# Cross-attention: the maxima of two score tiles subtracted by four 32-row matmuls behind the product passes of both

## The chip, the cores and the metric

One core of one Trainium2 chip runs the whole kernel. The metric is the device time of one execution in microseconds (us); the median of the runs counts.

## What is computed

A decoder layer in post-norm form, float32, batch 4, 512 positions, width 256. Only the second of its three parts matters here:

```python
x = _layernorm(x + _L0_attn_ref(...))              # self-attention over the batch, and a dynamic convolution
x = _layernorm(x + _L0_xattn_ref(x, context, ...)) # cross-attention, this case
x = _layernorm(x + _L0_ffn_ref(...))               # mixture of 8 experts, 2 per token

def _L0_xattn_ref(x, context, w_q, w_kv, w_out, b_out):   # 16 heads of 64, context of 1601 rows
    q = (x @ w_q).reshape(b, n, HEADS, DIM_HEAD)
    kv = (context @ w_kv).reshape(b, m, 2, HEADS, DIM_HEAD)
    k, v = (kv[:, :, 0], kv[:, :, 1])
    attn = jnp.einsum('bnhd,bmhd->bhnm', q, k) * scale
    attn = jax.nn.softmax(attn, axis=-1)
    out = jnp.einsum('bhnm,bmhd->bnhd', attn, v).reshape(b, n, INNER)
    return out @ w_out + b_out
```

## The kernel before

The cross-attention works in 16 rounds, one for each batch and each quad of four heads. A round has two blocks, p = 0 and p = 1, one for each pair of heads. In a block the transposed scores of the pair (context rows on partitions, 512 queries in the free dimension) are made in 13 tiles of 128 context rows, t = 0 to 12; the last has 65 rows (MT, M_LAST). A tile is 2 x 512 elements wide, one PSUM bank for each head, and `ps_s` has room for two tiles, used in turn. One head of a pair lies on partitions 0 to 63 of `q` and `k`, the other on 64 to 127 (XD = 64), so each matmul of a tile uses 64 rows of the array.

Float32 products are made from rounded parts: k_hi q_hi, k_lo q_hi and k_hi q_lo. A fourth pass subtracts the row maximum of every query: `row_one` is 1 in rows 0 and 64, and `q_neg` holds the negated maxima in rows 0 and 64 and zeros elsewhere (L836 to L844). ScalarE exponentiates the tile from PSUM into one of seven `pexp` buffers (L942), TensorE multiplies it with V (PV, L856), and GpSimd adds it to `total` (L1001), from which RS (L910) makes the row sums by a matmul with ones.

All engines walk the same list of steps (`walk`), and each does its own part of a step in that order. `block` (L554) writes the list of a block; `one_round` joins two blocks and the rest:

- S (p, t): the score tile. PV (p, t): in twos behind every odd t from 3 on, for tiles t-3 and t-2; the last three tiles' at the end of the block.
- MX: matmuls of q_hi and k_hi (L887) over 402 context rows, for the maxima of the next block. VectorE reduces each (L1060, `parts`). They come in groups of two, one per head; MX_BEFORE and MX_BEHIND say how many groups stand before and behind each S: one behind every t from 1 on, one more before t = 4, 7, 10 and 12.
- SH (p): at the end of a block VectorE reduces `parts` to `negmax` (L1067), a matmul with the identity turns it (L895), and ScalarE writes `q_neg` (L972).
- K, Q, V: projections (L827), split by ScalarE (`k_hi`) and VectorE (`k_lo`). K chunks 0 and 1 and Q stand at the end of the block before, chunks 2 and 3 behind t = 1. V stands in block 1.
- R1 to R4: reciprocals of the sums (L1075), `att` (L1080), `att_hi` (L967, ScalarE, t = 8), `att_lo` (L1083, VectorE). OP: the output projection (L827) behind t = 9, added to X by VectorE (L1090).
- LDA, LDB, LDC: loads of weights and context by SyncE. WA (t = 10 of block 0), WB, CX (t = 5 and 8, only where the batch changes): their split into parts, ScalarE's `_hi` first, then `_lo` by GpSimd (or VectorE for the second half of the context).

RING_JOBS (K, Q, MX, SH, V, RS, OP) share three PSUM banks, `ps_ring`, in turn; `take_bank` waits until the job three before has been drained. Waits are on semaphores; `exp_done`, `pv_done` and `add_done` count exponentials, PVs and adds. Seven `pexp` buffers let ScalarE run up to six tiles ahead of PV and of the add.

Of the kernel before, what the change touches and what calls it, by code (L numbers as in the profile page):

```python
# [5 lines left out]
P = 128  # L6
# [10 lines left out]
NC = N // P  # L17
# [535 lines left out]
def block(p, more, maxima, tail):  # L553


    steps = []

    def some(k):
        for _ in range(k):
            if maxima:  # L560
                steps.extend(maxima.pop(0))

    for t in range(MT):
        some(MX_BEFORE[t])
        steps.append(("S", p, t))
        some(MX_BEHIND[t])
        before, behind = more.get(t, ((), ()))
        steps.extend(before)
        if t % 2 == 1 and t >= 3:
            steps += [("PV", p, t - 3), ("PV", p, t - 2)]  # L570
        steps.extend(behind)
    some(len(maxima))
    steps += [("PV", p, t) for t in range(MT - 3, MT)]
    return steps + tail
# [138 lines left out]
def cross_attention(nc, a, X, consts, loads, x1_hi, x1_lo):  # L713
    ctx_raw, wa_raw, wb_raw = loads.ctx_raw, loads.wa_raw, loads.wb_raw
    ident, ones = consts["ident"], consts["ones"]
    with ExitStack() as ctx:
# [57 lines left out]

        def user_before(p, t):

            return p * MT + t - (MT if t == MT - 1 else NPB if t < NPB - 1 else NPB - 1)
# [40 lines left out]
        def _(pe):  # L818
# [11 lines left out]
            def handle(i, n, st):  # L830
                kind = st[0]
                if kind == "S":
                    p, t = st[1:]
                    if t == 0:
                        r, c = n.job(("SH", p))
                        pe.wait_ge(drained[r], c)  # L836
                    need(pe, s["exp_done"], n.of("S") - 1)
                    m, ms = rows(t), slice(t * P, t * P + rows(t))
                    for q, (kk, qq) in enumerate(((k_hi[p][:, ms], q_hi[p]), (k_lo[p][:, ms], q_hi[p]),
                                                  (k_hi[p][:, ms], q_lo[p]), (row_one[:, 0:m], q_neg[p]))):  # L840
                        for h in range(2):
                            ins = nc.tensor.matmul(ps_s[0:m, t_of(n), h, :], kk[half(h)], qq[half(h), :],  # L842
                                                   start=q == 0, stop=q == 3)
                    ins.then_inc(s["scores_ready"], 1)  # L844
# [79 lines left out]
            def t_of(n):  # L924
                return n.here.get("S", 0) % 2

# [5 lines left out]
        def _(act):  # L932
            def handle(i, n, st):
                kind = st[0]
                if kind == "S":
                    p, t = st[1:]
                    act.wait_ge(s["scores_ready"], n.of("S") + 1)
                    m, buf, prev = rows(t), pexp_buffer(t), user_before(p, t)
                    first = n.before.get("S", 0)
                    need(act, s["pv_done"], first + prev + 1)  # L940
                    need(act, s["add_done"], n.before.get("ADD", 0) + adds_through(prev))
                    nc.scalar.activation(pexp[0:m, buf], ps_s[0:m, (p * MT + t) % 2], ACT.Exp, scale=XD ** -0.5)\  # L942
                        .then_inc(s["exp_done"], 1)
# [41 lines left out]
                elif kind == "WA":  # L985
                    act.wait_ge(s["wa_in"], 16 * n.of("LDA"))
                    nc.scalar.copy(wa_hi[:], wa_raw[:]).then_inc(s["wa_hi_done"], 1)  # L987
                elif kind == "WB":
                    act.wait_ge(s["wb_in"], 16 * n.of("LDB"))
                    nc.scalar.copy(wb_hi[:], wb_raw[:]).then_inc(s["wb_hi_done"], 1)  # L990
# [35 lines left out]
        def _(dve):  # L1026
# [3 lines left out]
            for h in range(2):  # L1030
                nc.vector.memset(att[h * XD:h * XD + 1, 0:P], 1.0).then_inc(s["zero_set"], 1)
            dve.wait_ge(s["zero_set"], 3)
            nc.vector.tensor_copy(row_one[:], att[:, 0:P]).then_inc(s["ones_set"], 1)

            def handle(i, n, st):
# [26 lines left out]
                elif kind == "SH":  # L1062
# [3 lines left out]
                    for h, col in ((0, 0), (1, XD)):  # L1066
                        nc.vector.tensor_reduce(negmax[:, :, col:col + 1], parts[:, h], AX.X, ALU.max, negate=True)\  # L1067
# [598 lines left out]
```

## Time and profile before

| | |
|---|---|
| median of 3 runs | 2050.33 us (2050.1 to 2056.19) |
| profiled execution | 2053.94 us, span from first to last instruction 2052.2 us |
| TensorE (PE) matmuls | 1746.8 us busy, 85% |
| PEld (weight loads) | 1212.3 us, 59% |
| VectorE (DVE) | 1191.0 us, 58% |
| ScalarE (ACT) | 832.0 us, 41% |
| GpSimd (POOL) | 1323.0 us, 64% |
| mean granted TensorE clock | 0.919 |

The busy share of an engine is a mean over stages with different limits: the self-attention and the experts lie before and behind the sixteen rounds. A row of a timeline merges like instructions that follow each other (x2, x8) and gives the start of the first. Matmuls overlap in the array: the length of a row has the way through the array in it, and the difference between the starts of two rows is what a step costs TensorE. A time in square brackets is idle time before the row, with what ended it. Shapes of a matmul are written rows*columns of the array that its weights use, then what streams through.

### The profile page before, as it was taken

What the parts mean: (1) busy time and instruction counts of PE and PEld (TensorE: products, weight loads), DVE (VectorE), ACT (ScalarE), POOL (GpSimd) and SP (SyncE); (2) the same over time, 40 slices, a digit from 0 to 9 for tenths busy, and PEclk for the clock granted to TensorE, in tenths of its full rate; (3) what the DMA queues carried; (4) which work ended last, traced back from release to release, by engine and by line L of the source; (5) the groups of instructions that cost most, each with busy time, mean ns of one, the idle gap of its engine ahead of it and who ended that gap; (6) DMA issues with size and microseconds to landing.
All of it is one profiled execution on the core that took longest, in us unless ns stands there. A gap on an engine that the chain in (4) does not pass through costs nothing. (4 is left out here: it accounts for less than half of the span.)

```text
span 2052.2 us, 32755 instructions
## 1 busy us (share of the span) xinstructions
PE 1746.8 (85%) x10682; PEld 1212.3 (59%) x10682; DVE 1191.0 (58%) x2046; ACT 832.0 (41%) x1228; POOL 1323.0 (64%) x711
## 2 busy tenths in 40 slices
PE   7553599999989999998999999899999998509990
PEld 5443466666656666665666666566666664408980
DVE  4788555556565656556565665655565654553345
ACT  3111234444444444444444444444444444224440
POOL 2988338577676667576776676675766677454544
PEclk8775689999999999999999999999999999559995
DMA  5000200000200000010000001000000000321223
GB/s 185 1 21 24 79 1 22 1 22 0 73 1 22 22 3 22 0 52 22 21 1 23 1 21 52 21 22 1 21 1 21 15 1 1 124 84 63 71 63 128
DMA packets 37813, 68.09 MB, mean 33 GB/s; under 512 B 3560, under 2 KB 27504, under 8 KB 36656
## 3 DMA queue, kind: packets, MB, share of 16 engines
q1 hardware_dynamic: 33936, 56.12, 8.1%
q0 software_dynamic: 3744, 10.23, 1.5%
q8 instruction: 80, 1.31, 0.3%
q14 instruction: 53, 0.43, 0.1%
HBM read 52.84 MB, written 13.50 MB: 32 GB/s over the span
## 5 line engine op out<-in xcount | busy, mean ns | idle before, releaser
L1001 POOL TENSOR_TENSOR xa_total<-xa_total,xa_pexp 128x1024 f32<-128x1024 f32 (+1 forms) x352 | 852.9, 2423 | 52.7 <-ACT xa_pexp L942 27.3
L1060 DVE TENSOR_REDUCE xa_parts<-ps_ring 128x1 f32<-128x402 f32 x1024 | 532.3, 565 | 299.8 <-PE ps_ring L887 292.8
L942 ACT ACTIVATE xa_pexp<-ps_s 128x1024 f32<-128x1024 f32 (+1 forms) x416 | 422.7, 1025 | 419.0 <-PE ps_s L842 391.9
L856 PE MATMUL ps_pv<-xa_pexp,xa_v 128*64 128x512 f32 (+1 forms) x1664 | 399.8, 604 | 0.0
L887 PE MATMUL ps_ring<-xa_k_hi,xa_q_hi 64*128 64x402 f32 x1024 | 235.0, 377 | 32.7 <-DVE xa_parts L1060 31.4
L856 PEld LDWEIGHTS ps_pv<-xa_pexp,xa_v 128*64 128x64 f32 (+1 forms) x1664 | 106.2, 137 | 181.9 <-issue 148.3
L887 PEld LDWEIGHTS ps_ring<-xa_k_hi,xa_q_hi 64*128 64x128 f32 x1024 | 142.7, 186 | 118.2 <-DVE xa_parts L1060 58.9
L1001 POOL TENSOR_TENSOR xa_total<-xa_pexp 128x1024 f32<-128x1024 f32 x32 | 76.3, 2384 | 190.9 <-ACT xa_pexp L942 189.6
L1048 DVE TENSOR_TENSOR xa_k_lo<-ps_ring,xa_k_hi 128x402 fp32r<-128x402 f32 (+1 forms) x128 | 73.6, 575 | 214.7 <-ACT xa_k_hi L953 214.7
L842 PE MATMUL ps_s<-xa_q_hi,xa_k_hi 64*128 64x512 f32 (+1 forms) x832 | 194.0, 433 | 3.6 <-DVE xa_k_lo L1048 2.8
L842 PE MATMUL ps_s<-xa_q_neg,xa_row_one 64*128 64x512 f32 (+1 forms) x832 | 174.4, 393 | 0.0
L842 PE MATMUL ps_s<-xa_q_hi,xa_k_lo 64*128 64x512 f32 (+1 forms) x832 | 173.7, 392 | 0.0
L842 PE MATMUL ps_s<-xa_q_lo,xa_k_hi 64*128 64x512 f32 (+1 forms) x832 | 173.5, 391 | 0.0
L977 ACT COPY xa_v<-ps_ring 128x256 f32<-128x256 f32 (+1 forms) x208 | 77.4, 372 | 207.5 <-PE ps_ring L827 205.6
L1016 POOL TENSOR_TENSOR xa_wa_lo<-wa_raw,xa_wa_hi 128x1536 fp32r<-128x1536 f32 x17 | 59.0, 3473 | 145.5 <-ACT xa_wa_hi L987 145.5
L1075 DVE RECIPROCAL xa_inv<-xa_sums 128x128 f32<-128x128 f32 x128 | 119.9, 940 | 27.8 <-ACT xa_sums L964 27.8
L842 PEld LDWEIGHTS ps_s<-xa_q_hi,xa_k_hi 64*128 64x128 f32 (+1 forms) x832 | 80.3, 182 | 59.7 <-issue 35.6
L827 PEld LDWEIGHTS ps_ring<-xa_wa_hi,xa_ctx_hi 128*128 128x128 f32 (+1 forms) x416 | 63.1, 188 | 66.6 <-issue 60.8
L827 PE MATMUL ps_ring<-xa_wa_hi,xa_ctx_hi 128*128 128x256 f32 (+1 forms) x416 | 96.7, 314 | 0.1
L842 PEld LDWEIGHTS ps_s<-xa_q_neg,xa_row_one 64*128 64x128 f32 (+1 forms) x832 | 86.1, 181 | 16.0
L842 PEld LDWEIGHTS ps_s<-xa_q_lo,xa_k_hi 64*128 64x128 f32 (+1 forms) x832 | 85.9, 181 | 16.0
L953 ACT CAST xa_k_hi<-ps_ring 128x402 fp32r<-128x402 f32 (+1 forms) x128 | 63.2, 494 | 74.5 <-PE ps_ring L827 74.5
(263 smaller groups left out, 2946.2 us busy)
## 6 DMA issues: line engine op xcount, KB each, us to landing
wa_raw<-in_pack_a SPq DMA_DIRECT2D x17, 768.0 KB, 4.4
ex_w_raw<-in_pack_e SPq DMA_DIRECT2D x8, 1026.0 KB, 5.3
ctx_raw<-in_ctxT SPq DMA_DIRECT2D x4, 1601.0 KB, 8.5
wb_raw<-in_pack_b SPq DMA_DIRECT2D x16, 256.0 KB, 2.6
ex_w_hi<-ybuf SPq DMA_DIRECT2D x8, 512.0 KB, 7.6
sa_xT<-in_xT SPq DMA_DIRECT2D x8, 256.0 KB, 6.4
X<-in_x SPq DMA_DIRECT2D x1, 2048.0 KB, 11.5
x_hi<-sa_x1s_hi SPq DMA_DIRECT2D x16, 128.0 KB, 2.1
```

What stands on the lines that cost most here:

```text
L827: ins = nc.tensor.matmul(out, w, x, start=q == 0, stop=q == len(terms) - 1)
L842: ins = nc.tensor.matmul(ps_s[0:m, t_of(n), h, :], kk[half(h)], qq[half(h), :], start=q == 0, stop=q == 3)
L856: ins = nc.tensor.matmul(ps_pv[half(h), :], v[0:m, t, at:at + XD], pexp[0:m, buf, h, :], start=t == 0, stop=t == MT - 1)
L887: nc.tensor.matmul(ps_ring[:, r, 0:CW], q_hi[p][half(h), q * P:(q + 1) * P], k_hi[p][half(h), KC0[c]:KC0[c] + CW], start=True, stop=True)\
L942: nc.scalar.activation(pexp[0:m, buf], ps_s[0:m, (p * MT + t) % 2], ACT.Exp, scale=XD ** -0.5)\
L953: nc.scalar.copy(k_hi[p][:, KC0[c] + skip:KC0[c] + CW], ps_ring[:, r, skip:CW])\
L977: nc.scalar.copy(v[0:rows(t), t, :], ps_ring[0:rows(t), r, 0:4 * XD]).then_inc(drained[r], 1)
L1001: nc.gpsimd.tensor_tensor(total[p][0:m], first, pexp[0:m, buf], ALU.add).then_inc(s["add_done"], 1)
L1016: nc.gpsimd.tensor_tensor(wa_lo[:], wa_raw[:], wa_hi[:].bitcast(F32), ALU.subtract)\
L1048: nc.vector.tensor_tensor(k_lo[p][:, cols], ps_ring[:, r, skip:CW], k_hi[p][:, cols].bitcast(F32), ALU.subtract).then_inc(drained[r], 1)
L1060: nc.vector.tensor_reduce(parts[:, h, q, c:c + 1], ps_ring[:, r, 0:CW], AX.X, ALU.max)\
L1075: nc.vector.reciprocal(inv[:, cs], sums[:, cs]).then_inc(s["inv_ready"], 1)
```

## The change

The step S keeps only the three product passes of a tile. The subtraction becomes a step of its own, SX, behind the S of every odd tile and of the last one. It subtracts from both tiles of the pair at once, with one matmul per tile and head, each on its own 32 rows of the array: rows 0 and 32 for the two heads of the even tile, rows 64 and 96 for those of the odd tile. Each writes a PSUM bank of its own. For the last tile, alone, there are two. For this `row_one` has ones in rows 0, 32, 64 and 96, and `negmax` holds each head's maxima in two places, which the two reductions of SH write with doubled size. ScalarE waits for SX and does the exponentials of both tiles one after the other. The score matmuls no longer wait for `q_neg`, SX does. ScalarE's split of WA gets a wait for the output projection of block 1 that stands behind t = 9, because the exponential that used to keep it behind that projection has moved.

```diff
--- before.py
+++ after.py
@@ -563,6 +563,8 @@
     for t in range(MT):
         some(MX_BEFORE[t])
         steps.append(("S", p, t))
+        if t % 2 == 1 or t == MT - 1:
+            steps.append(("SX", p, t - t % 2))
         some(MX_BEHIND[t])
         before, behind = more.get(t, ((), ()))
         steps.extend(before)
@@ -771,6 +773,12 @@
 
         def half(p64):
             return slice(0, XD) if p64 == 0 else slice(XD, P)
+
+        def buf_of(p, t):
+            return (p * MT + t) % 2
+
+        def shifted_with(t):
+            return (t,) if t == MT - 1 else (t, t + 1)
 
         def user_before(p, t):
 
@@ -831,17 +839,24 @@
                 kind = st[0]
                 if kind == "S":
                     p, t = st[1:]
+                    need(pe, s["exp_done"], n.of("S") - 1)
+                    m, ms = rows(t), slice(t * P, t * P + rows(t))
+                    for q, (kk, qq) in enumerate(((k_hi[p][:, ms], q_hi[p]), (k_lo[p][:, ms], q_hi[p]),
+                                                  (k_hi[p][:, ms], q_lo[p]))):
+                        for h in range(2):
+                            nc.tensor.matmul(ps_s[0:m, buf_of(p, t), h, :], kk[half(h)], qq[half(h), :],
+                                             start=q == 0, stop=False)
+                elif kind == "SX":
+                    p, t = st[1:]
                     if t == 0:
                         r, c = n.job(("SH", p))
                         pe.wait_ge(drained[r], c)
-                    need(pe, s["exp_done"], n.of("S") - 1)
-                    m, ms = rows(t), slice(t * P, t * P + rows(t))
-                    for q, (kk, qq) in enumerate(((k_hi[p][:, ms], q_hi[p]), (k_lo[p][:, ms], q_hi[p]),
-                                                  (k_hi[p][:, ms], q_lo[p]), (row_one[:, 0:m], q_neg[p]))):
-                        for h in range(2):
-                            ins = nc.tensor.matmul(ps_s[0:m, t_of(n), h, :], kk[half(h)], qq[half(h), :],
-                                                   start=q == 0, stop=q == 3)
-                    ins.then_inc(s["scores_ready"], 1)
+                    both = shifted_with(t)
+                    for g, (u, h) in enumerate((u, h) for u in both for h in range(2)):
+                        at, m = slice(32 * g, 32 * g + 32), rows(u)
+                        ins = nc.tensor.matmul(ps_s[0:m, buf_of(p, u), h, :], row_one[at, 0:m], q_neg[p][at, :],
+                                               start=False, stop=True)
+                    ins.then_inc(s["scores_ready"], len(both))
                 elif kind == "PV":
                     p, t = st[1:]
                     if t == 0:
@@ -921,9 +936,6 @@
                         ins = project(ps_ring[:, r, q * E:(q + 1) * E], terms)
                     ins.then_inc(filled[r], 1)
 
-            def t_of(n):
-                return n.here.get("S", 0) % 2
-
             pe.wait_ge(s["ones_set"], 1)
 
             walk(pe, handle)
@@ -932,15 +944,16 @@
         def _(act):
             def handle(i, n, st):
                 kind = st[0]
-                if kind == "S":
-                    p, t = st[1:]
-                    act.wait_ge(s["scores_ready"], n.of("S") + 1)
-                    m, buf, prev = rows(t), pexp_buffer(t), user_before(p, t)
+                if kind == "SX":
+                    p = st[1]
+                    act.wait_ge(s["scores_ready"], n.of("S"))
                     first = n.before.get("S", 0)
-                    need(act, s["pv_done"], first + prev + 1)
-                    need(act, s["add_done"], n.before.get("ADD", 0) + adds_through(prev))
-                    nc.scalar.activation(pexp[0:m, buf], ps_s[0:m, (p * MT + t) % 2], ACT.Exp, scale=XD ** -0.5)\
-                        .then_inc(s["exp_done"], 1)
+                    for t in shifted_with(st[2]):
+                        m, buf, prev = rows(t), pexp_buffer(t), user_before(p, t)
+                        need(act, s["pv_done"], first + prev + 1)
+                        need(act, s["add_done"], n.before.get("ADD", 0) + adds_through(prev))
+                        nc.scalar.activation(pexp[0:m, buf], ps_s[0:m, buf_of(p, t)], ACT.Exp, scale=XD ** -0.5)\
+                            .then_inc(s["exp_done"], 1)
                 elif kind == "PV" and st[2] == MT - 1:
                     act.wait_ge(s["pv_done"], n.of("PV") + 1)
                     need(act, s["att_done"], n.of("R2"))
@@ -983,6 +996,9 @@
                         act.wait_ge(filled[r], c)
                     nc.scalar.copy(ctx_hi[:, k], ctx_raw[:, k]).then_inc(s["ctx_hi_done"], 1)
                 elif kind == "WA":
+                    if ("OP", 1, 1, 1) in n.jobs:
+                        r, c = n.job(("OP", 1, 1, 1))
+                        act.wait_ge(filled[r], c)
                     act.wait_ge(s["wa_in"], 16 * n.of("LDA"))
                     nc.scalar.copy(wa_hi[:], wa_raw[:]).then_inc(s["wa_hi_done"], 1)
                 elif kind == "WB":
@@ -1027,9 +1043,9 @@
             nc.vector.memset(negmax[:], 0.0)
             nc.vector.memset(att[:], 0.0).then_inc(s["zero_set"], 1)
             dve.wait_ge(s["zero_set"], 1)
-            for h in range(2):
-                nc.vector.memset(att[h * XD:h * XD + 1, 0:P], 1.0).then_inc(s["zero_set"], 1)
-            dve.wait_ge(s["zero_set"], 3)
+            for g in range(4):
+                nc.vector.memset(att[32 * g:32 * g + 1, 0:P], 1.0).then_inc(s["zero_set"], 1)
+            dve.wait_ge(s["zero_set"], 5)
             nc.vector.tensor_copy(row_one[:], att[:, 0:P]).then_inc(s["ones_set"], 1)
 
             def handle(i, n, st):
@@ -1063,8 +1079,9 @@
                     p = st[1]
                     r, c = n.job(("MX", p, 3, 1, NC - 1))
                     dve.wait_ge(drained[r], c)
-                    for h, col in ((0, 0), (1, XD)):
-                        nc.vector.tensor_reduce(negmax[:, :, col:col + 1], parts[:, h], AX.X, ALU.max, negate=True)\
+                    for h in range(2):
+                        nc.vector.tensor_reduce(negmax[:, :, 32 * h::XD].rearrange("p q g -> p g q"),
+                                                parts[:, h].unsqueeze(1).broadcast_to([P, 2, NC, 4]), AX.X, ALU.max, negate=True)\
                             .then_inc(s["shift_ready"], 1)
                 elif kind == "R1":
                     if st[2] == 0:
```

## Rows read from the trace of the kernel before

**Rows 1.** Two rounds as stretches: length, busy PE, PEld, DVE, ACT, POOL, PE clock, DMA

```profile
409.90:501.60 91.70, 89.19 (x564) 58.94 (x562) 54.06 (x95) 42.61 (x59) 62.45 (x27) 1.00 0.03 12
501.60:593.30 91.70, 83.87 (x532) 55.52 (x532) 57.58 (x92) 43.08 (x57) 61.62 (x25) 0.96 0.12 41
```

**Rows 2.** List of TensorE's waits: who waited for whom, us in total, times, longest

```profile
PE ps_ring L887 <- DVE xa_parts L1060: 31.4, 73, 0.6
```

**Rows 3.** Timeline of TensorE, K projections and then tile 0: start, length, engine, line, operation

```profile
409.26 0.53 PE L827 MATMUL ps_ring<-xa_ctx_hi,xa_wa_lo 128*128 128x402 f32 x2
409.63 0.53 PE L827 MATMUL ps_ring<-xa_ctx_lo,xa_wa_hi 128*128 128x402 f32 x2
410.09 0.50 PE L842 MATMUL ps_s<-xa_q_hi,xa_k_hi 64*128 64x512 f32 x2
410.43 0.39 PE L842 MATMUL ps_s<-xa_q_hi,xa_k_lo 64*128 64x512 f32 x2
410.66 0.40 PE L842 MATMUL ps_s<-xa_q_lo,xa_k_hi 64*128 64x512 f32 x2
```

**Rows 4.** The same timeline at t = 4 and 5 of block 1, and V

```profile
422.92 0.35 PE L887 MATMUL ps_ring<-xa_k_hi,xa_q_hi 64*128 64x402 f32 x2
423.11 0.40 PE L842 MATMUL ps_s<-xa_q_hi,xa_k_hi 64*128 64x512 f32 x2
...
424.03 0.35 PE L887 MATMUL ps_ring<-xa_k_hi,xa_q_hi 64*128 64x402 f32 x2
424.31 1.94 PE L856 MATMUL ps_pv<-xa_pexp,xa_v 128*64 128x512 f32 x8
426.18 0.50 PE L827 MATMUL ps_ring<-xa_wa_hi,xa_ctx_hi 128*128 128x256 f32 x2
426.52 0.40 PE L827 MATMUL ps_ring<-xa_wa_lo,xa_ctx_hi 128*128 128x256 f32 x2
426.76 0.40 PE L827 MATMUL ps_ring<-xa_wa_hi,xa_ctx_lo 128*128 128x256 f32 x2
```

**Rows 5.** The same timeline, row sums behind t = 3 of a block 0

```profile
559.51 1.08 PE L910 MATMUL ps_ring<-xa_total,ones 128*64 128x512 f32 x4 [0.17 <-DVE xa_parts L1060]
```

**Rows 6.** The same timeline, from the maxima behind t = 6 to those behind t = 7

```profile
428.83 0.52 PE L887 MATMUL ps_ring<-xa_k_hi,xa_q_hi 64*128 64x402 f32 x3
429.84 0.45 PE L887 MATMUL ps_ring<-xa_k_hi,xa_q_hi 64*128 64x402 f32 x1 [0.49 <-DVE xa_parts L1060]
...
430.95 0.34 PE L887 MATMUL ps_ring<-xa_k_hi,xa_q_hi 64*128 64x402 f32 x1
431.61 0.44 PE L887 MATMUL ps_ring<-xa_k_hi,xa_q_hi 64*128 64x402 f32 x1 [0.32 <-DVE xa_parts L1060]
```

**Rows 7.** Timelines of VectorE and TensorE at t = 9 of block 0

```profile
481.22 2.31 DVE L1080 TENSOR_TENSOR xa_att<-xa_pv_sb,xa_inv 128x512 f32<-128x512 f32 x1 [0.19 <-DVE xa_inv L1075]
...
484.08 0.44 PE L887 MATMUL ps_ring<-xa_k_hi,xa_q_hi 64*128 64x402 f32 x1 [0.56 <-DVE xa_parts L1060]
```

**Rows 8.** Timelines of VectorE and TensorE at t = 10 of block 0

```profile
488.91 3.23 DVE L1060 TENSOR_REDUCE xa_parts<-ps_ring 128x1 f32<-128x402 f32 x6
...
489.58 0.42 PE L887 MATMUL ps_ring<-xa_k_hi,xa_q_hi 64*128 64x402 f32 x2
```

**Rows 9.** Page, costliest groups: busy us, mean ns of one, idle us before

```profile
L942 ACT ACTIVATE xa_pexp<-ps_s 128x1024 f32<-128x1024 f32 (+1 forms) x416 | 422.7, 1025 | 419.0 <-PE ps_s L842 391.9
```

**Rows 10.** Timelines of ScalarE, VectorE and TensorE, t = 8 and 9 where the batch changes

```profile
575.00 1.52 ACT L984 CAST xa_ctx_hi<-ctx_raw 128x1601 fp32r<-128x1601 f32 x1
...
576.55 3.71 DVE L1040 TENSOR_TENSOR xa_ctx_lo<-ctx_raw,xa_ctx_hi 128x1601 fp32r<-128x1601 f32 x1 [1.31 <-ACT xa_ctx_hi L984]
...
583.06 0.58 PE L827 MATMUL ps_ring<-xa_wa_hi,xa_att_hi 128*128 128x256 f32 x1 [5.94 <-DVE xa_att_lo L1083]
```

**Rows 11.** Timelines of GpSimd and TensorE in the last round

```profile
1704.72 3.48 POOL L1016 TENSOR_TENSOR xa_wa_lo<-wa_raw,xa_wa_hi 128x1536 fp32r<-128x1536 f32 x1 [8.96 <-ACT xa_wa_hi L987]
...
1721.00 1.97 PE L910 MATMUL ps_ring<-xa_total,ones 128*64 128x512 f32 x4 [5.09 <-POOL xa_total L1001]
```

## The prediction

> **What bounds the kernel now.** I read the stretches by round first. A round of the cross-attention (four heads, one batch) takes 91.70 us, and TensorE has a matmul in flight for 89.19 us of it; a round in which the batch changes also takes 91.70 us, but TensorE is busy for only 83.87 us [rows 1]. So TensorE's own order sets the time, and what the change does to the sum of its steps is what it does to the kernel, except where TensorE already waits. The list of waits names the commonest one: maxima matmuls (L887) that wait for VectorE's reduction to free a ring slot, 73 times and 31.4 us in all [rows 2]. Then I read TensorE's timeline around the score tiles for the price of a pass and of a change between kinds of matmul, and last the three places where an extra step can disappear in a wait.
>
> **Prices.** A pass over one tile is two matmuls of 64 rows, side by side. Starts are 0.23 us apart (410.43 to 410.66), and 0.19 us for the 402 columns of a maxima pair (422.92 to 423.11) [rows 3, 4]. Score passes and maxima pairs follow each other with nothing between. Not so where the shape of the array changes. The 128-row passes of K are 0.37 us apart (409.26 to 409.63), but the next 64-row pass starts 0.46 us after the last (0.09 more), and that first pass takes 0.34 us instead of 0.23 (0.11 more), its weight load not being ahead of it [rows 3]. From a maxima pair to PV (128 rows, 64 columns) it is 0.28 us instead of 0.19, again 0.09 more, and the first V pass behind PV takes 0.34 us against 0.24 for the next (0.10 more) [rows 4]. So every change of shape seen here costs 0.09 us of emptying and 0.10 to 0.11 us of bare weight load: 0.2 us.
>
> **What is removed.** Per tile one pass of two 64-row matmuls, 0.23 us: 0.46 us for two tiles, 32 blocks of 13 tiles.
>
> **What is added.** Per block seven SX steps: six of four 32-row matmuls, and one for tile 12 of two. No row of before has a 32-row matmul, so its price has to be bounded. The matmuls themselves: if the four run side by side they take a pass, 0.23 us, or 0.25 with two more instructions (the pair takes 0.02 us more than 512 columns at 2.4 GHz, 0.213 us); if only two at a time do, 0.46 us. I take 0.25, because 64-row pairs already run side by side into separate banks. The changes of shape, 64 to 32 rows and back: at least nothing, if the array sees 32-row and 64-row groups as one shape; at most what each change costs in rows 3 and 4, 0.09 + 0.11 + 0.09 + 0.10 = 0.39 us. I take the upper end: the nearest rows are changes in row count (128 to 64) and in columns (128 to 64), and both cost the same.
>
> The Trainium skill speaks against this change at that point ("TensorEngine Tiling (Array Packing)", Key Properties): changing the tiling mode, not just the tile, drains the engine. The trace agrees for 128 and 64 rows (0.09 us before, 0.11 us after); no row shows 64 and 32. On the side-by-side run, "TensorE: Matmul & The Clock Gate", Part 3, gives 3.07 times for four 32-row matmuls of 512 columns; as an estimate from that page they would take 4 x 0.213 / 3.07 = 0.28 us, which would make the sum 5 us longer.
>
> **Pair by pair.** An undisturbed pair of tiles gives -0.46 + 0.25 + 0.39 = +0.18 us; the single tile 12 gives -0.23 + 0.23 + 0.39 = +0.39 us. But SX stands before a maxima pair, and where that pair waits for VectorE anyway the extra goes into the wait:
> - t = 1 and 5: nothing waits, +0.18 each.
> - t = 3: the row sums behind it wait 0.17 us for a ring slot [rows 5]; the extra goes in there. 0.
> - t = 7: two maxima pairs stand before tile 7. The fourth matmul waits 0.49 us, the sixth 0.32 us (430.95 to 431.61 instead of side by side), both by VectorE's row of four reductions, which starts with the maxima behind tile 6 [rows 6]. The pass taken from tile 6 starts that row 0.23 us earlier, and what SX adds before the fifth matmul (0.09 + 0.25 + 0.11 + 0.09 for a pass of 0.23: 0.31 us) is hidden by the wait of 0.6 us before the sixth. -0.23.
> - t = 9: ordinary in block 1, +0.18. In block 0 the second maxima matmul behind tile 9 waits 0.56 us, because VectorE is 2.31 us in `att` [rows 7]: hidden, 0.
> - t = 11: VectorE's six reductions start at 488.91, so the first ends about 489.45; the maxima pair behind tile 10, at 489.58, meets no wait now, but 0.23 us earlier it would, and the tile behind a wait has its first pass bare (+0.11). So the pass taken from tile 10 wins some 0.05 us at best; with +0.31 before the last maxima pair the pair of tiles gives +0.3 [rows 8].
> - t = 12: no wait, +0.39.
>
> Block 1: 0.18 + 0 + 0.18 - 0.23 + 0.18 + 0.3 + 0.39 = +1.0. Block 0: 0.18 + 0 + 0.18 - 0.23 + 0 + 0.3 + 0.39 = +0.82. Sixteen of block 0 and fifteen of block 1 (the last has no maxima and is held by GpSimd) give 13.1 + 15.0 = +28.1 us.
>
> **What moves on the other engines.** ScalarE's exponentials now come in twos, behind SX. The even tile's starts about 1.1 us later (a maxima pair, three passes and SX, less the pass that it no longer has: 0.19 + 0.69 + 0.09 + 0.36 - 0.23). Who needs it? The tile two further on needs its score bank: between SX and that tile lie a maxima pair and PV (1.87 us, 424.31 to 426.18 [rows 4]) or two K chunks, and one exponential is 1.03 us [rows 9]. Hidden, except in the last block at t = 1, where some 0.6 us shows before a wait for GpSimd that is longer. PV of a tile comes a pair later, hidden. The copy of K chunk 2 stands behind both exponentials and comes 0.5 us later, its reader one tile later: hidden, 0 to 0.2 us per block.
>
> Steps at even t now stand on ScalarE's queue ahead of that tile's exponential. Two of them matter. CX 1 and R3 at t = 8, in the three rounds where the batch changes: today `ctx_hi` starts at 575.00 behind the exponential of tile 8, VectorE idles 1.31 us for it (576.55), `att_lo` stands behind that 3.71 us, and TensorE waits 5.94 us until 583.06 [rows 10]. Without that exponential `ctx_hi` is done before VectorE has reduced tile 8's maxima, so the chain comes 1.31 + 0.23 = 1.5 us earlier: 3 x -1.5 = -4.6 us. The second is WA at t = 10. It gets a wait for the projection OP behind tile 9, so nothing that would run is queued behind it for long (the next is SX 10), and it still starts some 2.5 us earlier than now (by the maxima pair and the tile between OP and its present place, 0.6 and 0.9 us, and an exponential). GpSimd idles 8.96 us for it before `wa_lo` in the last round, and its adds then hold TensorE for 5.09 us [rows 11]; 2.5 us less of that, against 1.1 us by which the even exponentials feed its adds later: -1.5 us at the end. VectorE's SH reductions double in size, two short instructions per block under three tiles of PV: 0. The set-up memsets: 0.
>
> **Sum.** +28.1 - 4.6 - 1.5 = +22.0 us. The profiled execution took 2053.94 us for a span of 2052.2; the median of three is 2050.33, 0.2% lower. The steps are the same in both, so I add them to the median: 2072.3 us.
>
> **Rivals.**
> 1. *The array takes 32- and 64-row groups as one shape (faster).* Then the place is the same SX, its price 0.25 us without 0.39, and the pair -0.21. It decides as soon as the two changes together cost less than 0.21 us, as 0.46 - 0.25 is what is saved. Against it: 0.2 us at every change in rows 3 and 4. For it: none of these is between two kinds of row group. Block 1: four pairs and t = 7 at -0.21, t = 11 and 12 at 0 = -1.05; block 0, where t = 9 is held by VectorE: -0.84. 16 x -0.84 + 15 x -1.05 - 6.1 = -35 us: 2015 us. Chance 0.13.
> 2. *Half the price*, 0.2 us for both changes (the weight loads of free row groups run ahead, or the emptying is short). Ordinary pairs -0.01, t = 7 -0.23, t = 11 +0.12, t = 12 +0.2: about 0 a block, and -6 from the other engines: 2043 us. Chance 0.09.
> 3. *It doesn't do what it says*: the four run two by two. Another 0.21 us for each pair that no wait hides (five in block 1, four in block 0), 9 x 16 x 0.21 = +30: 2102 us. Chance 0.06.
> 4. My forecast, 2072 us, own range 2058 to 2086 (t = 3, 9 and 11 hidden or not, some hundredths on SX, the 6 us of the other engines): 0.72.
>
> **Range and chances.** 2040 to 2090 leaves out the free change and the serial run, 19 in 100. A measurement here tells about 0.3% (6 us) from nothing. Faster by more than that: the first rival and half of the second, 0.18. Within: the other half and the low tail of the forecast, 0.08. Slower: 0.74.
>
> **What will show it.** SX: starts of the pass before, of SX and of the maxima pair behind it, 0.32 and 0.45 us apart (0.23 and 0.25 if the change is free, over 0.6 if two by two), and a maxima pair that lasts 0.38 instead of 0.28 to PV. The wait before the sixth maxima matmul at t = 7 shrinks from 0.32 to almost nothing. `att_lo` wait 4.4 instead of 5.9 us. A round of 93.5 us. I am wrong if the rounds get shorter, or if TensorE shows waits for `pexp` between pairs.

## The result, and the profile after

The changed kernel takes 2071.56 us (median of 5 runs, 2067.63 to 2074.92), the kernel before 2050.76 us over the same five rounds. The ratio is 1.0099, with a 95% interval of 1.0087 to 1.0111: about 21 us slower. The forecast was 2072, slower. The profiled execution took 2073.53 us for a span of 2071.6 us.

| | before | after |
|---|---|---|
| span of the profiled execution | 2052.2 us | 2071.6 us |
| TensorE busy | 1746.8 us | 1792.4 us |
| ScalarE busy | 832.0 us | 814.7 us |
| first SH matmul starts at | 275.85 us | 277.38 us |
| second SH matmul starts at | 313.91 us | 317.19 us |
| last SH matmul starts at | 1709.63 us | 1732.18 us |

TensorE's timeline after, at t = 0 and 1 of a block 1. The columns are those of [rows 3], which it answers: start, length, engine, line, operation. The stage starts here at another time than in the profile of before, so compare differences of starts only.

```profile
415.71 0.39 PE L847 MATMUL ps_s<-xa_q_hi,xa_k_hi 64*128 64x512 f32 x2
415.94 0.39 PE L847 MATMUL ps_s<-xa_q_hi,xa_k_lo 64*128 64x512 f32 x2
416.17 0.40 PE L847 MATMUL ps_s<-xa_q_lo,xa_k_hi 64*128 64x512 f32 x2
416.50 0.50 PE L857 MATMUL ps_s<-xa_q_neg,xa_row_one 32*128 32x512 f32 x4
416.93 0.45 PE L902 MATMUL ps_ring<-xa_k_hi,xa_q_hi 64*128 64x402 f32 x2
417.31 0.64 PE L835 MATMUL ps_ring<-xa_ctx_hi,xa_wa_hi 128*128 128x402 f32 x2
```

The last product pass stands 0.33 us before SX where passes are 0.23 us apart: 0.10 us of emptying. SX, four matmuls, takes 0.43 us to the maxima pair. That pair takes 0.38 us to the K projection; at the same place before it took 0.27 us: its weight load is bare. So the array takes 32 and 64 rows as two shapes, and each change costs what it costs between 64 and 128. The row of all four matmuls of SX is 0.50 us long, no longer than that of two bare 64-row matmuls (0.50 at 414.90 in the same timeline): the four run side by side. Taking the emptying (0.09) and the bare load (0.11) of before off the 0.43 us leaves 0.23 us for them, as an estimate.

One normal block 0 and one block 1 as stretches from SH to SH, of after and then of before (columns as in [rows 1]):

```profile
366.29:410.23 43.94, 43.37 (x262) 25.25 (x260) 27.60 (x47) 19.92 (x26) 25.44 (x11) 1.00 0.00 1
410.23:459.44 49.21, 48.72 (x304) 30.25 (x302) 26.71 (x47) 21.54 (x33) 37.15 (x17) 1.00 0.07 23
```

```profile
361.88:405.39 43.51, 41.88 (x262) 26.86 (x260) 27.12 (x47) 20.42 (x26) 22.85 (x10) 1.00 0.00 1
405.39:453.64 48.25, 47.34 (x304) 32.05 (x302) 26.93 (x47) 22.19 (x33) 40.10 (x18) 1.00 0.07 23
```

Block 0 is 0.43 us longer and block 1 0.96 us. The twelve normal blocks 0 are 0.41 to 0.61 us longer but one of 0.25, and the fifteen blocks 1 0.96 to 1.12. The very first block, with no attention of an earlier round beside it, is 1.76 us longer. The 31 blocks from the first SH to the last add up to +21.0 us. The rest of the difference is +1.5 us ahead of the first SH and -3.1 us behind the last. The list of TensorE's waits after, which answers [rows 2] and [rows 10]:

```profile
PE ps_ring L835 <- DVE xa_att_lo L1100: 17.9, 4, 6.3
PE ps_ring L902 <- DVE xa_parts L1076: 15.1, 31, 0.5
```

The waits for the maxima's reduction that this list shows have halved, from 31.4 us (73 times) to 15.1 us (31 times). Part of what SX costs has gone into them. And TensorE is busy 45.6 us more although it runs the same 10682 matmuls over the same columns. By the page a subtraction matmul lasts 490 ns on average where it lasted 393, and a maxima matmul 423 where it lasted 377: I read this as waits for weights and for VectorE that are counted as busy.

### The profile page after: what moved, and what is told of

It is laid out like the page before. It is cut to its first block and busy times, and to the rows that moved or that the text cites. A ratio compares the mean times of both kernels' runs of the same rounds, so it can differ in the third digit from the quotient of the medians.

```text
span 2071.6 us, 32489 instructions
## 1 busy us (share of the span) xinstructions
PE 1792.4 (87%) x10682; PEld 1159.5 (56%) x10682; DVE 1194.3 (58%) x2048; ACT 814.7 (39%) x1228; POOL 1327.1 (64%) x711
## 5 line engine op out<-in xcount | busy, mean ns | idle before, releaser
L955 ACT ACTIVATE xa_pexp<-ps_s 128x1024 f32<-128x1024 f32 (+1 forms) x416 | 405.0, 1022 | 465.6 <-PE ps_s L857 462.4
L902 PE MATMUL ps_ring<-xa_k_hi,xa_q_hi 64*128 64x402 f32 x1024 | 260.9, 423 | 16.5 <-DVE xa_parts L1076 15.1
L902 PEld LDWEIGHTS ps_ring<-xa_k_hi,xa_q_hi 64*128 64x128 f32 x1024 | 126.6, 186 | 147.0 <-issue 83.1
L847 PE MATMUL ps_s<-xa_q_hi,xa_k_hi 64*128 64x512 f32 (+1 forms) x832 | 202.0, 439 | 3.6 <-issue 2.5
L857 PE MATMUL ps_s<-xa_q_neg,xa_row_one 32*128 32x512 f32 (+1 forms) x832 | 111.5, 490 | 0.0
L847 PEld LDWEIGHTS ps_s<-xa_q_lo,xa_k_hi 64*128 64x128 f32 (+1 forms) x832 | 89.1, 181 | 15.1
L847 PEld LDWEIGHTS ps_s<-xa_q_hi,xa_k_lo 64*128 64x128 f32 (+1 forms) x832 | 89.6, 182 | 3.0
L857 PEld LDWEIGHTS ps_s<-xa_q_neg,xa_row_one 32*128 32x128 f32 (+1 forms) x832 | 40.9, 177 | 84.0 <-issue 73.3
## 6 DMA issues: line engine op xcount, KB each, us to landing
X<-in_x SPq DMA_DIRECT2D x1, 2048.0 KB, 11.5
```

Source lines behind the costliest of these rows:

```text
L847: nc.tensor.matmul(ps_s[0:m, buf_of(p, t), h, :], kk[half(h)], qq[half(h), :], start=q == 0, stop=False)
L857: ins = nc.tensor.matmul(ps_s[0:m, buf_of(p, u), h, :], row_one[at, 0:m], q_neg[p][at, :], start=False, stop=True)
L902: nc.tensor.matmul(ps_ring[:, r, 0:CW], q_hi[p][half(h), q * P:(q + 1) * P], k_hi[p][half(h), KC0[c]:KC0[c] + CW], start=True, stop=True)\
L955: nc.scalar.activation(pexp[0:m, buf], ps_s[0:m, buf_of(p, t)], ACT.Exp, scale=XD ** -0.5)\
```

## Experiments

**The 64-row version.** SX stays where it is, but subtracts with one 64-row pass per tile; the maxima lie in two rows as before. So the order of all engines is that of the changed kernel, without the change of shape and without the saved pass. Shortened: the set-up of `row_one` and the reductions of SH go back to their form before.

```diff
-                    for g, (u, h) in enumerate((u, h) for u in both for h in range(2)):
-                        at, m = slice(32 * g, 32 * g + 32), rows(u)
-                        ins = nc.tensor.matmul(ps_s[0:m, buf_of(p, u), h, :], row_one[at, 0:m], q_neg[p][at, :],
+                    for u, h in ((u, h) for u in both for h in range(2)):
+                        m = rows(u)
+                        ins = nc.tensor.matmul(ps_s[0:m, buf_of(p, u), h, :], row_one[half(h), 0:m], q_neg[p][half(h), :],
```

> The kernel after the change, with its maxima subtracted in the same place but by two passes of 64-row matmuls, one per tile, instead of one of 32 rows. If the loss is the change of the array's shape around SX (my theory), each pair loses 0.25 + 0.39 us of matmuls and gains 0.46, tile 12 loses 0.39: no block is longer than before on TensorE's account, and what is left is what the new order on ScalarE gives, some 6 to 14 us: 2036 to 2046 us. If the loss comes from the exponentials in twos, the time stays at 2068 to 2076 us.

Measured: 2036.72 us, ratio to before 0.9926 (0.9911 to 0.9942): 14 us faster than before and 35 us faster than the changed kernel. The timeline of this version at the same place as above:

```profile
413.24 0.40 PE L847 MATMUL ps_s<-xa_q_lo,xa_k_hi 64*128 64x512 f32 x2
413.48 0.62 PE L857 MATMUL ps_s<-xa_q_neg,xa_row_one 64*128 64x512 f32 x4
413.93 0.34 PE L902 MATMUL ps_ring<-xa_k_hi,xa_q_hi 64*128 64x402 f32 x2
414.21 0.64 PE L835 MATMUL ps_ring<-xa_ctx_hi,xa_wa_hi 128*128 128x402 f32 x2
```

No gap before the subtraction (0.24), two passes in 0.45 us, and the maxima pair takes 0.28 us. From the last product pass to K it is 0.97 us here and 1.14 us in the changed kernel: four 64-row matmuls one pair behind the other cost 0.17 us less than four 32-row ones all at once. The theory holds, and the rival is out.

**ScalarE's order alone.** The matmuls of the kernel before, each with its fourth pass; only the exponentials move.

```diff
+        if t % 2 == 1 or t == MT - 1:
+            steps.append(("SX", p, t - t % 2))
...
-                if kind == "S":
-                    p, t = st[1:]
-                    act.wait_ge(s["scores_ready"], n.of("S") + 1)
+                if kind == "SX":
+                    p = st[1]
+                    act.wait_ge(s["scores_ready"], n.of("S"))
...
+                    if ("OP", 1, 1, 1) in n.jobs:
+                        r, c = n.job(("OP", 1, 1, 1))
+                        act.wait_ge(filled[r], c)
```

> The kernel before, its matmuls in their order untouched (the fourth pass in each tile), but ScalarE does both exponentials of two tiles at the odd one, as after the change, with the wait of WA. It shows the part of the other engines alone. My theory: shorter by 6 to 14 us, 2036 to 2045 us, through the context's split and att_hi that no longer stand behind an exponential (rows 10) and the earlier split of WA. The rival (twos are what costs): 2060 us or more, with waits of TensorE for pexp.

Measured: 2042.73 us, ratio 0.9957 (0.9945 to 0.9969), 8 us faster than before. The twos are no cost; what they do is a small gain. By blocks it is mixed, and both at t = 9: a normal block 0 is 0.75 us shorter, and a block 1 is 0.6 us longer, because a V projection there now waits 0.55 us for VectorE's `parts`. VectorE walks the same order as before, but `att_lo`, which stands ahead of tile 9's maxima, takes 2.88 us instead of 1.80. The kernel before, then this one:

```profile
438.33 1.80 DVE L1083 TENSOR_TENSOR xa_att_lo<-xa_att,xa_att_hi 128x512 fp32r<-128x512 f32 x1 [0.41 <-ACT xa_att_hi L967]
...
433.62 2.88 DVE L1095 TENSOR_TENSOR xa_att_lo<-xa_att,xa_att_hi 128x512 fp32r<-128x512 f32 x1
```

Why the length of such an instruction differs is answered below, under t = 9. From the first SH to the last it is -5.7 us. The first SH itself came 3.2 us earlier, which is no effect of the edit (see below).

**The suspected price twice as often.** The fourth pass of the kernel before, in its place, on 32 rows for each head.

```diff
+                            at = half(h) if q < 3 else slice(h * XD, h * XD + 32)
-                            ins = nc.tensor.matmul(ps_s[0:m, t_of(n), h, :], kk[half(h)], qq[half(h), :],
+                            ins = nc.tensor.matmul(ps_s[0:m, t_of(n), h, :], kk[at], qq[at, :],
```

> The kernel before with one edit: the two matmuls of the fourth pass use 32 rows of the array each instead of 64 (rows 0 to 31 and 64 to 95, where their data lies). Nothing is removed or moved, the same number of matmuls stream the same columns, and the changes of shape come 13 times per block instead of 7. My theory: 0.39 us for each tile less some 1.2 us per block that waits hide, 31 x 3.9 = 120 us: 2150 to 2190 us. If 32 and 64 rows are one shape to the array: 2050 us.

Measured: 2171.28 us, ratio 1.0583 (1.0562 to 1.0604), +120 us. Its timeline at t = 3:

```profile
430.15 0.40 PE L843 MATMUL ps_s<-xa_q_lo,xa_k_hi 64*128 64x512 f32 x2
430.48 0.49 PE L843 MATMUL ps_s<-xa_q_neg,xa_row_one 32*128 32x512 f32 x2
430.90 0.45 PE L888 MATMUL ps_ring<-xa_k_hi,xa_q_hi 64*128 64x402 f32 x2
431.28 1.08 PE L911 MATMUL ps_ring<-xa_total,ones 128*64 128x512 f32 x4
```

From the start of the two 32-row matmuls to the maxima it is 0.42 us, where four took 0.43. The same columns stream as before, so the loss comes from the shape. This kernel has 13 steps of another shape in a block, the changed kernel 7.

**SX behind the maxima pair.** The same four 32-row matmuls one step later, where the next step (K, RS, PV) has a shape of its own anyway.

```diff
-        if t % 2 == 1 or t == MT - 1:
-            steps.append(("SX", p, t - t % 2))
         some(MX_BEHIND[t])
+        if t % 2 == 1 or t == MT - 1:
+            steps.append(("SX", p, t - t % 2))
```

> The kernel after the change with SX moved behind the maxima pair that followed it. What comes next there (K, RS, PV) has another shape than both, so one of the two added changes falls away. My theory: 0.2 us less for each of seven SX in 31 blocks, less what waits take, 30 to 43 us under the kernel after: 2028 to 2042 us, now below before. The rival (twos and their delay cost): 2070 us or more, since the exponentials come 0.2 us later still.

Measured: 2092.37 us, ratio 1.02 (1.0185 to 1.0215). Wrong by 50 us, and on the rival's side. But the rival asks for waits on `pexp`, and of those TensorE has one of 1.1 us, as in the changed kernel. Its list of waits has another at its head:

```profile
PE ps_ring L902 <- DVE xa_parts L1076: 42.7, 73, 1.1
```

Where nothing waits, the one change of shape is saved: at t = 1 the pair of tiles is 0.20 us shorter than in the changed kernel. The loss sits at t = 7 and t = 9. The timeline of a block 0 there, TensorE and then VectorE:

```profile
479.64 0.44 PE L902 MATMUL ps_ring<-xa_k_hi,xa_q_hi 64*128 64x402 f32 x1 [0.55 <-DVE xa_parts L1076]
480.02 0.51 PE L857 MATMUL ps_s<-xa_q_neg,xa_row_one 32*128 32x512 f32 x4
480.46 1.94 PE L871 MATMUL ps_pv<-xa_pexp,xa_v 128*64 128x512 f32 x8
...
485.38 0.45 PE L902 MATMUL ps_ring<-xa_k_hi,xa_q_hi 64*128 64x402 f32 x1 [1.04 <-DVE xa_parts L1076]
...
482.09 2.76 DVE L1097 TENSOR_TENSOR xa_att<-xa_pv_sb,xa_inv 128x512 f32<-128x512 f32 x1 [0.19 <-DVE xa_inv L1092]
```

The maxima pair now stands in front of SX, nothing keeps it from VectorE, and it waits for its ring slot; then SX is paid in full behind that wait. In front of the maxima SX was hidden in such waits. At t = 7 this costs 0.43 us a block, at t = 9 of a block 0 another 1.0 us. Two more things make it dear. `att` takes 2.76 us here and 1.69 in the changed kernel (see t = 9 below). And in 8 of the 31 blocks the granted clock falls after the two waits at t = 7, so that PV runs at 1.2 GHz and takes 3.47 us where it takes 1.94 at 2.4 GHz (the second row is a stretch, columns as in [rows 1], with the granted clock of 0.50):

```profile
526.59 3.47 PE L871 MATMUL ps_pv<-xa_pexp,xa_v 128*64 128x512 f32 x8
526.90:530.20 3.30, 3.30 (x9) 0.70 (x6) 2.75 (x3) 1.89 (x2) 3.19 (x2) 0.50 0.95 346
```

TensorE had stood for 0.49 and 0.55 us shortly before. In the changed kernel the clock falls only where the batch changes, three times between the second SH and the last, as in the kernel before. Eight times some 1.6 us is 13 us of the 21 by which this version is slower than the changed one.

**The same three orders with VectorE out of the way.** To test that, VectorE reads only half of the context rows for the maxima, so these three kernels leave half of the maxima's input out; everything else is theirs.

```diff
-                    nc.vector.tensor_reduce(parts[:, h, q, c:c + 1], ps_ring[:, r, 0:CW], AX.X, ALU.max)\
+                    nc.vector.tensor_reduce(parts[:, h, q, c:c + 1], ps_ring[:, r, 0:CW // 2], AX.X, ALU.max)\
```

The kernel before:

> The kernel before, but VectorE's maxima read only 201 of the 402 columns (half of the context rows are left out of the maxima; all matmuls stay). Its reductions take some 0.35 us instead of 0.565, so the waits before maxima matmuls nearly vanish. Base for the two beside it. 2005 to 2030 us.

The changed kernel:

> The kernel after the change with the same shortened maxima (half of the context rows left out of them). With no waits to hide SX, the plain sum must show: 6 x 0.18 + 0.39 = 1.47 us per block, 31 blocks, +46 us, less some 6 us from the other engines: 36 to 46 us over the shortened kernel before. If waits hid nothing of SX, the distance stays what it is without the edit, some 21 us.

SX behind the maxima:

> SX behind the maxima pair (the version that took 2092 us), with the same shortened maxima. If that version was slow because SX no longer stands in front of the waits for VectorE and is paid in full behind them, it is now faster than the shortened kernel after by one change of shape per SX, 7 x 0.2 x 31 = 43 us (35 to 45), and within 10 us of the shortened kernel before. If SX behind the maxima is dear in itself, it stays 15 us or more above the shortened kernel after.

Measured: 2008.14 us (2006.49 to 2009.67), 2041.36 us (2039.98 to 2042.23) and 2003.87 us (2003.24 to 2004.48). SX behind the maxima is now 37 us faster than SX in front, and 4 us faster than the shortened kernel before. So it was slow because of VectorE and what followed its waits, and not in itself. That 37 is near the 43 that one change of shape less per SX asks is partly luck: per pair at t = 1, 5 and 11 it is 0.18 to 0.20 us, but t = 9 alone gives 20 of the 37 us, through an `att` of 0.69 us instead of 2.23 in blocks 0 and shorter waits where the batch changes. That waits hid part of SX is seen at t = 3: SX costs nothing there in the changed kernel, and 0.17 to 0.19 us with the shortened maxima. The changed kernel's distance to before grows from 21 to 33 us, under the 36 to 46 expected. One wait of 0.49 us before tile 7 has become 0.28 us and has not gone, and the base has kept one behind PV at t = 9 of block 1 that the other lacks:

```profile
428.46 0.51 PE L827 MATMUL ps_ring<-xa_wa_hi,xa_ctx_hi 128*128 128x256 f32 x2 [0.34 <-DVE xa_parts L1060]
```

At t = 9 of a block 0 it is the other way round (+0.71 us instead of the plain 0.18), as `att` takes 1.03 us in the base and 2.23 in the changed kernel. None of the three has a fall of the clock between the second SH and the last except where the batch changes.

**Moving the maxima off the wait.** The 64-row version with the maxima group before tile 7 moved to before tile 8.

```diff
-MX_BEFORE = (0, 0, 0, 0, 1, 0, 0, 1, 0, 0, 1, 0, 1)
+MX_BEFORE = (0, 0, 0, 0, 1, 0, 0, 0, 1, 0, 1, 0, 1)
```

> The 64-row version of the change (2037 us) with the maxima group before tile 7 moved to before tile 8, behind PV. Theory: the wait of 0.49 us and the bare first pass (0.11) behind it go in every block with maxima, and part of the wait before the sixth matmul: 0.6 to 1.0 us x 31: 2006 to 2018 us. If those waits only come back at tile 8 or 9: 2030 us or more.

Measured: 2051.44 us (2043.03 to 2055.95), ratio 0.999 (0.9976 to 1.0005): 15 us lost against the 64-row version. The wait at tile 7 is gone and a longer one has come at tile 8:

```profile
432.71 0.34 PE L902 MATMUL ps_ring<-xa_k_hi,xa_q_hi 64*128 64x402 f32 x1
434.06 0.45 PE L902 MATMUL ps_ring<-xa_k_hi,xa_q_hi 64*128 64x402 f32 x1 [1.01 <-DVE xa_parts L1076]
```

There the maxima queue behind `att` on VectorE; in blocks 0 the same wait is 2.14 us. My expectation had looked at TensorE's queue and not at what else VectorE has at that step. In ten of the twelve normal blocks 0 the granted clock falls in or right behind that wait, and the passes then start 0.42 us apart instead of 0.23. The stretch behind it, with a granted clock of 0.50:

```profile
480.40:483.80 3.40, 3.08 (x13) 2.54 (x13) 2.68 (x6) 0.49 (x2) 2.00 (x1) 0.50 0.00 0
```

Such a block takes 45.0 us or more, and the two without a fall 43.4 and 43.5. As an estimate, ten times 1.5 us of lower clock is the whole 15 us lost against the 64-row version. The 64-row version stays the fastest with the whole computation.

## Why the prediction was right

Prices of one step, in us:

| term of the sum | predicted | measured |
|---|---|---|
| four 32-row matmuls | 0.25 | 0.23 (estimate from rows) |
| emptying before SX, after the last product pass | 0.09 | 0.10 |
| SX to maxima pair | 0.45 | 0.43 |

Differences between after and before, from the start of one even tile to the next, for one pair of tiles and summed over the 31 blocks:

| place | predicted, each | measured, each | predicted, sum | measured, sum |
|---|---|---|---|---|
| t = 1 | +0.18 | +0.17 | 5.6 | 5.5 |
| t = 3 | 0 | -0.02 | 0 | -0.5 |
| t = 5 | +0.18 | +0.40 | 5.6 | 12.5 |
| t = 7 | -0.23 | -0.22 | -7.1 | -6.7 |
| t = 9, block 1 | +0.18 | -0.03 | 2.7 | -0.5 |
| t = 9, block 0, without the next line | 0 | -0.54 | 0 | -6.3 |
| t = 9 where the batch changes, three | -1.5 | -1.50 to -1.63 | -4.6 | -4.7 |
| t = 11 | +0.3 | +0.38 | 9.3 | 11.9 |
| t = 12 | +0.39 | +0.33 | 12.1 | 10.2 |
| from SH to tile 0 | 0 | 0 | 0 | -0.3 |
| 31 blocks | | | 23.5 | 21.0 |
| end, behind the last SH | | | -1.5 | -3.1 |
| ahead of the first SH | | | 0 | +1.5 |

**The deciding step was right.** No row of before showed 32 rows, and the prediction took the price of the nearest changes of shape for it. The timeline of after shows that price, the 64-row version takes it away (-35 us), and the version with 32 rows in every tile, which has it 13 times in a block instead of 7, costs +120 us. The rivals of a free and of a half-priced change are out; so is the one of matmuls two by two, by the one row of 0.50 us for all four. The Trainium skill's rule ("TensorEngine Tiling (Array Packing)", Key Properties: changing the tiling mode drains the engine) holds here for 32 against 64 rows as well, and the row shows what the rule doesn't say: the weight load bare behind the emptying costs as much again. The estimate from the Trainium skill, "TensorE: Matmul & The Clock Gate", Part 3, 0.28 us for the four, is above the 0.23 us worked out from the rows here.

Of the other signs that the prediction named, the round is 93.15 us (93.5 forecast) and the wait for `att_lo` 3.87 us (4.4). The wait before the sixth maxima matmul at t = 7 has gone from the list, but part of it stays inside the pair: that pair takes 0.64 us to PV (436.47 to 437.11) and not 0.38.

**t = 5 was too small by 0.22 us, and the term that failed is "nothing waits".** The timeline after, t = 4 and 5 of a block 0:

```profile
477.40 0.57 PE L902 MATMUL ps_ring<-xa_k_hi,xa_q_hi 64*128 64x402 f32 x2
477.61 0.60 PE L847 MATMUL ps_s<-xa_q_hi,xa_k_hi 64*128 64x512 f32 x2
477.95 0.50 PE L847 MATMUL ps_s<-xa_q_hi,xa_k_lo 64*128 64x512 f32 x2
478.18 0.49 PE L847 MATMUL ps_s<-xa_q_lo,xa_k_hi 64*128 64x512 f32 x2
478.61 0.51 PE L857 MATMUL ps_s<-xa_q_neg,xa_row_one 32*128 32x512 f32 x4
```

The pass taken from tile 4 brings the maxima pair behind it so near to VectorE's reductions that its second matmul waits a little (the row is 0.57 us long, not 0.35). Then tile 5's first pass takes 0.34 us instead of 0.23, and the last one 0.43 us to SX instead of 0.33. In the 64-row version t = 5 costs 0.24 us too, where its plain sum is 0, so 32 rows are not the cause. I read this as one head's half of the array running some 0.1 us behind the other's, which costs nothing until the array has to be empty. It is what I had counted at t = 11, at a place where I had not looked. With the shortened maxima the stretch from the maxima pair before tile 4 to PV goes from 2.61 us (kernel before) to 2.79 us (changed kernel): the plain sum. So the wait as its cause is shown; the reading of the 0.1 us is not.

**t = 9 of block 0 was too large by 0.54 us,** the term "hidden, 0". What the maxima pair there waits for, `att` on VectorE, is shorter itself (compare [rows 7]). GpSimd's add beside `att`, before and then after, with VectorE and TensorE after:

```profile
480.60 2.39 POOL L1001 TENSOR_TENSOR xa_total<-xa_total,xa_pexp 128x1024 f32<-128x1024 f32 x1
...
486.06 2.39 POOL L1017 TENSOR_TENSOR xa_total<-xa_total,xa_pexp 128x1024 f32<-128x1024 f32 x1 [0.74 <-ACT xa_pexp L955]
487.31 1.69 DVE L1097 TENSOR_TENSOR xa_att<-xa_pv_sb,xa_inv 128x512 f32<-128x512 f32 x1 [0.19 <-DVE xa_inv L1092]
489.32 0.67 PE L902 MATMUL ps_ring<-xa_k_hi,xa_q_hi 64*128 64x402 f32 x2
489.92 1.94 PE L871 MATMUL ps_pv<-xa_pexp,xa_v 128*64 128x512 f32 x8
```

`att` takes 1.69 us instead of 2.31, and the pair to PV 0.60 us instead of 1.27. It comes with ScalarE's order: the kernel with that order alone has blocks 0 shorter by 0.75 us. Its length follows GpSimd. The add ends at 482.99 before and at 488.45 after, and `att` ends at 483.53 and 489.00: 0.54 and 0.55 us behind it. The prediction had the same row of 2.31 us but took its length as fixed. The ten profiles hold 320 `att`: 38 take 0.69 or 0.70 us, and each of the other 282, up to 2.87 us long, ends 0.54 to 0.56 us after the GpSimd instruction that ran when it started (an add in all but six). `att_lo` of block 1 in the kernel with ScalarE's order alone does so too: the add runs from 433.58 to 435.94, and it ends at 436.50. So ScalarE's new order moves the exponentials, they move the adds, and where the add ends sooner `att` does too. No run moved an add alone, so this is read from the rows.

**t = 9 of block 1 was too large by 0.21 us.** Up to PV the pair costs the +0.17 us forecast, but in the kernel before the second V projection behind it waited a little, and after it no longer does. Its first pass, before and then after, starts 0.36 and 0.23 us behind the pass before it, and has its weight load bare only before:

```profile
440.67 0.50 PE L827 MATMUL ps_ring<-xa_wa_hi,xa_ctx_hi 128*128 128x256 f32 x2
445.86 0.40 PE L835 MATMUL ps_ring<-xa_wa_hi,xa_ctx_hi 128*128 128x256 f32 x2
```

`att_lo`, which stands ahead of tile 9's maxima on VectorE, takes 0.90 us there instead of 1.80. So the prediction looked at the waits in front of PV and missed one behind it. Over the 31 blocks t = 5 and t = 11 came out 9.5 us above the forecast and t = 9 and t = 12 11.5 us below. That the total lies nearer than its terms is luck.

**Where the batch changes** the chain came forward as worked out: `ctx_hi` starts right behind the exponentials of tiles 6 and 7, VectorE no longer idles for it, and the wait of [rows 10] falls from 5.94 to 3.87 us. That is 2.1 us and not 1.5, mostly because `ctx_lo` takes 3.02 us instead of 3.71; it too ends at a fixed time behind GpSimd's add beside it, 1.69 us in both kernels.

```profile
579.87 1.53 ACT L997 CAST xa_ctx_hi<-ctx_raw 128x1601 fp32r<-128x1601 f32 x1
583.29 3.02 DVE L1056 TENSOR_TENSOR xa_ctx_lo<-ctx_raw,xa_ctx_hi 128x1601 fp32r<-128x1601 f32 x1
589.11 0.58 PE L835 MATMUL ps_ring<-xa_wa_hi,xa_att_hi 128*128 128x256 f32 x1 [3.87 <-DVE xa_att_lo L1100]
```

**The end gained 3.1 us, twice the forecast.** `wa_lo` starts 8.0 us before the last SH after and 4.9 before, 3.1 us earlier where 2.5 were forecast, and the 1.1 us by which the even exponentials come later didn't show: GpSimd's adds in the last block came forward by the whole 3.1 us. The first row sums there, before [rows 11], start 11.4 us behind the last SH; after, 8.3 us:

```profile
1740.45 1.08 PE L925 MATMUL ps_ring<-xa_total,ones 128*64 128x512 f32 x4 [1.63 <-POOL xa_total L1017]
```

**What lies ahead of the first SH is no part of the change.** Both kernels run the same projections and maxima there. From 260 to 280 us the granted clock was 0.78 of full speed before and 0.67 after:

```profile
260.00:280.00 20.00, 18.40 (x83) 14.61 (x84) 10.74 (x22) 3.86 (x10) 0.00 (x0) 0.78 0.00 1
```

```profile
260.00:280.00 20.00, 18.36 (x77) 13.93 (x76) 9.96 (x21) 3.56 (x9) 0.00 (x0) 0.67 0.00 1
```

TensorE stood at 1.2 GHz (0.50, from 260 to 270 us of after) and came back to 2.4 GHz later there; it was busy nearly without a gap before that in both. In the profiles of before, after and the first four experiments the first SH starts anywhere from 271.0 to 277.9 us. The kernels that hold the change are both the late and the early ones: the changed kernel 277.4, the version with SX behind the maxima 271.0. So some 7 us of scatter lie in a stage that the change doesn't touch, and single profiles should be compared from SH to SH.

## What to carry to other kernels

Packing small matmuls into row groups pays only if what it saves is more than the two changes of shape around it, here 0.39 us together, or 1.7 passes of 512 columns; look at what stands before and behind before you count the columns saved. A step added on the bound engine in front of a wait is partly hidden in it, and the same step behind the wait is paid in full, so a step that "saves a switch" by moving behind a wait can lose. Look at the granted clock behind every new wait: here it halved in some blocks and cost 1.5 us or more each time. And when a prediction takes a length from a row, ask what ran beside that row: a VectorE instruction beside a GpSimd add was as long as the add let it be. When a change has a main edit and a side effect on another engine's order, build each alone: here the side effect was a gain of 8 us under a loss, and the change without its main idea beats both kernels at 2036.72 us.

## What the hardware showed

- Four 32-row matmuls of 512 columns into four PSUM banks run side by side: one row of 0.50 us, and 0.43 us to the next step, against 0.42 us for two of them.
- From 64 to 32 rows costs 0.10 us of emptying and a bare weight load (about 0.1 us), and the way back the same again: 0.4 us for the two changes together.
- A small wait of one matmul of a side-by-side pair came with 0.1 us more in the next tile's first pass and another 0.1 us at the next change of shape (t = 5).
- VectorE's `att` (128x512 float32) takes 0.69 us or, in 282 of 320 cases, until 0.55 us after the end of the GpSimd instruction that ran when it started, up to 2.87 us in all.
- After waits of TensorE of 0.5 to 2.1 us the granted clock was 0.50 for some 3.4 us in 8 blocks of the version with SX behind the maxima and in 10 of the last one; PV took 3.47 us instead of 1.94.
